# Queries made for one head of two batches, 512 columns at once, instead of two heads of one batch

## The chip, the cores and the metric

The program runs on one core of a Trainium2 chip. Its time is the device time of one launch in microseconds. Three runs of the kernel before gave 613.03, 613.40 and 614.61 us; their median is 613.4 us.

## The reference

Two layers follow each other on x of 4 batches x 256 tokens x 256 features, float32. Each sublayer is followed by a residual sum and a layer norm:

```
x = layernorm(x + attention0(x))   # latent queries and keys, rotary part, causal, 16 heads
x = layernorm(x + experts(x))      # 16 experts, the best 2 of each token, silu
x = layernorm(x + attention1(x))   # 16 query heads, 4 key heads, rotary, alibi, 30*tanh(s/30), causal
x = layernorm(x + x @ sign(w)*mean|w| + bias)
```

What the change touches are the queries of both attentions. In layer 0 they are rmsnorm(x @ Wq_a) @ Wq_b, with Wkv_b's key part folded into Wq_b by the kernel, so that a head's queries have 64 latent and 64 rotary features. In layer 1 they are x @ Wq, 128 features a head. In both, the rotary step then multiplies them by a cosine and adds a swapped copy times a sine. The scores are queries times keys; each head of each batch has its own causal softmax over 256 tokens.

## The kernel before

Everything stays in SBUF with features in partitions. The 16 heads are taken as 8 pairs p, the 4 batches as b, and one unit of work is m = 4p + b. `steps` (L363 to L375) writes the attention loop of every engine: bodies n = 4p + b from 0 to 31 (pair 0 and pair 7 written out, pairs 1 to 6 in a hardware loop), and three bodies behind them that only finish. TensorE, VectorE, ScalarE and GpSimd each run their own list of instructions in order and meet at semaphores.

A unit of queries (`pe_queries`, L478) fills one PSUM bank of 128 x 512: both heads of the pair, 256 tokens of one batch each. Products of float32 parts are made in passes (a high and a low part of each operand): 5 matmuls for each head in layer 0, 6 in layer 1, each of 256 moving columns. In body n TensorE first makes the scores of body n, then the query unit n + 3 (`ahead`, L377), then the context products and transposes of earlier bodies. The units 0 to 2 are made ahead of the loop (`pe_first_queries`). From unit 3 on all units use bank 7, so a unit waits until the one before has been read.

Layer 0, after a unit is in the bank: VectorE multiplies it by the cosine into qT (`dve_cos`, L1241) and twice 32 rows by the sine into `swapped` (L1247), and GpSimd adds the two in qT (`pool_sin`, L1524) and raises q_ready. In a body the softmax runs as: VectorE takes the row maxima (L1281, L1282) and neg_max (L1284, 128 x 4 values, both operands in SBUF), ScalarE makes four exp (L935), VectorE the reciprocals (L1292), GpSimd the normalisation (L1536) and right behind it the addition on qT of unit n + 3. TensorE transposes the result one body later. At b = 0 ScalarE also splits the next pair's weights into w_hi (L908) and GpSimd makes w_lo (L1223).

Layer 1, after a unit is in the bank: ScalarE copies it with halves of the partitions swapped (L917, L918), GpSimd multiplies that by the sine (L1528), VectorE multiplies by the cosine (L1241) and adds into q_sum (L1256). One body later ScalarE rounds q_sum to q_hi (L963) and VectorE takes the rest as q_lo (L1262), which raises q_ready. Ahead of q_lo VectorE makes k_hi and k_lo of the keys (L1271, L1273). In a body ScalarE makes tanh (L972), GpSimd adds the mask (L1546, L1547), ScalarE makes the exp (L983). w_lo is VectorE's here (L1223, at b = 0); TensorE needs it for the next pair's first unit, in the body b = 1.

The scores of body n wait for q_ready (L510, L558): the count n + 1, that is, the unit of the same number. Layer 0 reads qT, layer 1 reads q_hi and q_lo, all of them 128 x (2 heads) x (4 x 256 tokens).

Of the kernel before, what the change touches and what calls it, by code (L numbers as in the profile page):

```python
# [12 lines left out]
ALU = mybir.AluOpType  # L13
ACT = mybir.ActivationFunctionType
AX_X = mybir.AxisListType.X

P = 128
# [76 lines left out]
def raw(ap):  # L94

    return ap.bitcast(F32)
# [8 lines left out]
def build(nc, a, out, ctx):  # L105
# [205 lines left out]
    def pair_view(ap):  # L311
        return ap.rearrange("p (h t) -> p h t", h=2)
# [11 lines left out]
    def query_bank(p, b):  # L324

        return 4 + b if isinstance(p, int) and p == 0 and b < 2 else QRY
# [106 lines left out]
    def pe_project_out(eng, at):  # L433

        turn, parts = (0, PAIRS) if at["layer"] == 0 else (2, H)
        for t in range(NT):
# [32 lines left out]
            if t == 5 and at["layer"] == 1:  # L469
# [5 lines left out]
                                           ffn_bw[:, o, k * P:k * P + P], ident[:])  # L475
                mm.then_inc(ff["bwT_done"], 1)

    def pe_queries(eng, at, p, b):  # L478

        m = 4 * p + b  # L480
        if b == 0:
            eng.wait_ge(at["w_hi_done"], p + 1)
            eng.wait_ge(at["w_lo_done"], p + 1)
        if not (isinstance(p, int) and m < 3):
            if at["layer"] == 0:
                eng.wait_ge(at["sin_done"], m)
            else:
                eng.wait_ge(at["cos_done"], m)
                eng.wait_ge(at["swap_done"], m)
        some = slice(T * b, T * b + T)  # L490
        for h in range(2):
            dst, head = bank[:, query_bank(p, b), h * T:h * T + T], slice(h * P, h * P + P)
            if at["layer"] == 0:
                three_pass(eng, dst, w_hi[:, 0, head], w_lo[:, 0, head], latT_hi[:, 0, some], latT_lo[:, 0, some],
                           True, False)

                eng.matmul(dst, w_hi[:, 1, head], latT_hi[:, 1, some], start=False, stop=False,
                           skip_group_check=True)
                mm = eng.matmul(dst, w_lo[:, 1, head], latT_hi[:, 1, some], start=False, stop=True,
                                skip_group_check=True)  # L500
            else:
                for k in range(2):
                    mm = three_pass(eng, dst, w_hi[:, k, head], w_lo[:, k, head], xT_hi[:, k, some],
                                    xT_lo[:, k, some], k == 0, k == 1)
        mm.then_inc(at["q_done"], 1)

    def pe_attention0(eng, at):
        def body(p, b, n, lag, own, more):
            if own:
                eng.wait_ge(at["q_ready"], n + 1)  # L510
                if lag(2):
                    eng.wait_ge(at["exp_done"], n - 1)
                for h in range(2):
                    dst = bank[:, 2 * (b % 2) + h, :]
                    q = qT[:, h, T * b:T * b + T]
                    eng.matmul(dst[:, 0:T], q[:, P:T], keysT[:, 0, T * b:T * b + T],  # L516
                               start=True, stop=False, skip_group_check=True)
                    eng.matmul(dst[:, T:T + P], q[:, 0:P], keysT[:, 0, T * b:T * b + P],
                               start=False, stop=False, skip_group_check=True)

                    mm = eng.matmul(dst[:, P:3 * P], ident_bf[:], mask_bf[:],  # L521
                                    start=False, stop=True, skip_group_check=True)
                mm.then_inc(at["scores_done"], 1)
            if own and ahead(p, b, more):
                pe_queries(eng, at, *ahead(p, b, more))
            if lag(2):
                b2 = (b - 2) % B
                eng.wait_ge(at["probsT_copied"], n - 1)
                if lag(3):
                    eng.wait_ge(at["ctx_copied"], n - 2)  # L530
                values = [key_tok[:, 2 * b2 + j, 0:KVL] for j in range(2)]
                for h in range(2):
                    pt = probsT[:, b % 2, h, :]
                    dst = bank[64 * h:64 * h + 64, CTX, 0:T]
                    eng.matmul(dst, values[0], pt[:, 0:T], start=True, stop=False, skip_group_check=True)
                    mm = eng.matmul(dst[:, P:T], values[1], pt[:, T:T + P],
                                    start=False, stop=True, skip_group_check=True)
                mm.then_inc(at["ctx_done"], 1)
            if lag(1):
                eng.wait_ge(at["probs_ready"], n)  # L540
                if lag(2):
                    eng.wait_ge(at["probsT_copied"], n - 1)
                for h in range(2):
                    pr = probs[:, (b - 1) % 2, h, :]
                    dst = probsT_bank[:, h, :]
                    eng.transpose(dst[:, 0:P], pr[:, T:T + P], ident[:])
                    eng.transpose(dst[:, P:T], pr[:, 0:P], ident[:])
                    mm = eng.transpose(dst[:, T:T + P], pr[:, P:T], ident[:])
                mm.then_inc(at["probsT_done"], 1)

        steps(eng, body)

    def pe_attention1(eng, at):

        def body(p, b, n, lag, own, more):
            par = b % 2
            if own:
                eng.wait_ge(at["q_ready"], n + 1)  # L558
                eng.wait_ge(at["k_copied"], n + 1)
                if lag(2):  # L560
                    eng.wait_ge(at["capped"], n - 1)
                for tile in range(2):
                    dst = bank[:, 2 * par + tile, 0:(2 - tile) * T]
                    keys = slice(tile * P, tile * P + P)
                    queries = slice(T * b + tile * P, T * b + T)
                    three_pass(eng, dst, k_hi[:, par, keys], k_lo[:, par, keys], q_hi[:, :, queries],
                               q_lo[:, :, queries], True, False)

                    mm = eng.matmul(dst, alibi_keys[:, keys], alibi_queries[:, bass.ds(2 * p, 2), tile * P:T],  # L569
                                    start=False, stop=True, skip_group_check=True)  # L570
                mm.then_inc(at["scores_done"], 1)
# [385 lines left out]
    def act_query_hi(act, at, p, b):  # L957

        m = 4 * p + b
        act.wait_ge(at["q_summed"], m + 1)  # L960
        if not (isinstance(p, int) and p == 0):
            act.wait_ge(at["scores_done"], m - 3)
        act.activation(q_hi[:, :, T * b:T * b + T], pair_view(q_sum[:, b % 2, :]), ACT.Copy).then_inc(at["q_hi_done"], 1)  # L963

    def act_attention1(act, at):
        def body(p, b, n, lag, own, more):
# [265 lines left out]
    def dve_cos(dve, at, p, b):  # L1232
        m = 4 * p + b
        if at["layer"] == 0:
            dve.wait_ge(at["q_done"], m + 1)
        else:
            dve.wait_ge(at["swap_done"], m + 1)
            if not (isinstance(p, int) and m < 2):
                dve.wait_ge(at["q_ready"], m - 1)
        dst = qT[:, :, T * b:T * b + T] if at["layer"] == 0 else pair_view(q_sum[:, b % 2, :])  # L1240
        dve.tensor_tensor(dst, pair_view(bank[:, query_bank(p, b), :]), cos_rows(at["layer"]),  # L1241
                          ALU.mult).then_inc(at["cos_done"], 1)
        if at["layer"] == 0:
            if not (isinstance(p, int) and m < 2):
                dve.wait_ge(at["q_ready"], m - 1)
            for to, of in ((64, 96), (96, 64)):
                ins = dve.tensor_tensor(pair_view(swapped[to:to + 32, b % 2, :]),  # L1247
                                        pair_view(bank[of:of + 32, query_bank(p, b), :]),
                                        rope_sin[of:of + 32, 0:1, :].broadcast_to([32, 2, T]), ALU.mult)
            ins.then_inc(at["sin_done"], 1)  # L1250
# [8 lines left out]
    def dve_query_lo(dve, at, p, b):  # L1259

        dve.wait_ge(at["q_hi_done"], 4 * p + b + 1)
        dve.tensor_tensor(q_lo[:, :, T * b:T * b + T], pair_view(q_sum[:, b % 2, :]),  # L1262
                          raw(q_hi[:, :, T * b:T * b + T]), ALU.subtract).then_inc(at["q_ready"], 1)

    def dve_keys(dve, at, p, b):

# [251 lines left out]
    def pool_sin(pool, at, p, b):  # L1518
        m = 4 * p + b
        if at["layer"] == 0:  # L1520
            q = qT[:, :, T * b:T * b + T]
            pool.wait_ge(at["cos_done"], m + 1)
            pool.wait_ge(at["sin_done"], m + 1)
            pool.tensor_tensor(q, q, pair_view(swapped[:, b % 2, :]), ALU.add).then_inc(at["q_ready"], 1)  # L1524
        else:
            pool.wait_ge(at["swap_done"], m + 1)
            sw = pair_view(swapped[:, b % 2, :])
            pool.tensor_tensor(sw, sw, sin_rows(), ALU.mult).then_inc(at["sin_done"], 1)  # L1528
# [233 lines left out]
```

## Time and profile before

| what | us |
|---|---|
| median of three runs | 613.4 |
| the profiled execution, its own time | 610.71 |
| its span | 609.0 |
| TensorE matmuls busy | 506.7 (83%) |
| VectorE busy | 410.6 (67%) |
| ScalarE busy | 343.4 (56%) |
| GpSimd busy | 306.8 (50%) |
| layer 0's loop, bodies 0 to 31: start of the scores | 38.9 to 179.1 |
| layer 1's loop, bodies 0 to 31: start of the scores | 382.4 to 527.5 |

A matmul's busy time reaches from its start to the end of its result, so that neighbours overlap; the distance of two starts is what one costs. PEld is the weight load, which runs beside the matmul before it. The start of a body's scores is read at its first weight load: of keysT and qT (L516) in layer 0, of q_hi and k_hi (L394) in layer 1. A row with x2 merges two instructions of one kind that follow each other.

### The profile page before, as it was taken

To read this page: it belongs to the slowest core of one execution; us is meant where nothing else is said; L and a number is where in the kernel's file an instruction comes from. 1 tells how busy PE (TensorE), PEld (TensorE's weight loads), DVE (VectorE), ACT (ScalarE), POOL (GpSimd) and SP (SyncE) were. 2 spreads that over 40 slices of the span, in tenths; PEclk is the share of its full clock that TensorE was granted. 3 is DMA by queue.
4 is the path that set the end of the run, shared out by engine and by line. 5 is a ranking of instruction groups with operands and counts; after the bars stand their busy time and mean duration, and the time that the engine had idled before them with its cause. 6 is when DMAs were issued, how large, how long until landed. Compare 5 with 4: busy or idle time off the path is not lost. (4 is left out here: it accounts for less than half of the span.)

```text
span 609.0 us, 11070 instructions
## 1 busy us (share of the span) xinstructions
PE 506.7 (83%) x3497; PEld 442.3 (73%) x3513; DVE 410.6 (67%) x883; ACT 343.4 (56%) x737; POOL 306.8 (50%) x304
## 2 busy tenths in 40 slices
PE   5878999999986866278990479899999999879983
PEld 5567888888865866257870357788988888779983
DVE  2666888888863765424552766788888888585765
ACT  4534777676784432133340156888888888745313
POOL 5726686766752022532336555566666666570110
PEclk9997999999996967569996599999999999979997
DMA  8949995000000044246532200000000000400002
GB/s 282 350 127 399 425 427 223 0 0 0 1 1 1 1 150 195 70 153 225 160 114 86 78 0 1 2 2 0 0 0 0 0 0 1 138 18 2 1 1 69
DMA packets 19170, 56.34 MB, mean 93 GB/s; under 512 B 2773, under 2 KB 12507, under 8 KB 15419
## 3 DMA queue, kind: packets, MB, share of 16 engines
q1 hardware_dynamic: 15616, 47.41, 20.8%
q0 software_dynamic: 3520, 8.51, 4.3%
q8 instruction: 18, 0.29, 0.2%
q14 instruction: 16, 0.12, 0.1%
HBM read 27.98 MB, written 28.18 MB: 92 GB/s over the span
## 5 line engine op out<-in xcount | busy, mean ns | idle before, releaser
L935 ACT ACTIVATE probs<-bank,neg_max,q_scale 128x256 f32<-128x256 f32 (+1 forms) x128 | 63.6, 506 | 34.5 <-DVE neg_max L1284 34.4
L1536 POOL TENSOR_TENSOR probs<-probs,inv_sum 128x512 f32<-128x512 f32 x64 | 52.3, 839 | 44.7 <-DVE inv_sum L1292 44.4
L394 PE MATMUL bank<-xT_hi,w_hi 128*128 128x256 f32 (+1 forms) x144 | 46.2, 321 | 11.0 <-DVE w_lo L1223 4.8
L1546 POOL TENSOR_TENSOR probs<-probs,tables 128x256 f32<-128x256 f32 x32 | 26.8, 839 | 48.3 <-ACT probs L972 48.3
L1528 POOL TENSOR_TENSOR swapped<-swapped,tables 128x512 f32<-128x512 f32 x32 | 42.3, 1323 | 12.1 <-ACT swapped L918 12.1
L1247 DVE TENSOR_TENSOR swapped<-bank,tables 32x512 f32<-32x512 f32 x64 | 44.4, 693 | 1.4
L1524 POOL TENSOR_TENSOR qT<-qT,swapped 128x512 f32<-128x512 f32 x32 | 40.8, 1275 | 7.1 <-DVE swapped L1247 7.1
L395 PE MATMUL bank<-xT_lo,w_hi 128*128 128x256 f32 (+1 forms) x144 | 43.1, 299 | 0.0
L396 PE MATMUL bank<-xT_hi,w_lo 128*128 128x256 f32 (+1 forms) x144 | 43.1, 299 | 0.0
L1618 POOL DMA_INDIRECT slots<-x_tok,slot x16 | 15.8, 990 | 53.5 <-DVE slot L1453 49.8
L516 PE MATMUL bank<-keysT,qT 128*128 128x256 f32 x128 | 39.2, 389 | 0.7 <-ACT wo_full L1048 0.7
L396 PE MATMUL bank<-wo_hi,ctx_lo 128*128 128x256 f32 x128 | 39.4, 308 | 0.0
L394 PEld LDWEIGHTS bank<-xT_hi,w_hi 128*128 128x128 f32 x144 | 28.0, 194 | 14.9 <-issue 11.8
L1628 POOL DMA_DIRECT2D slots<-y_slot x31 | 16.8, 543 | 43.1 <-DVE y_slot L1491 42.4
L1649 POOL TENSOR_TENSOR x_tok<-x_tok,tables 128x512 f32<-128x512 f32 x8 | 15.0, 1888 | 41.0 <-PE bank L402 41.0
L730 PE MATMUL bank<-gu_all,xgT 128*128 x124 | 34.6, 404 | 0.0
L1547 POOL TENSOR_TENSOR probs<-probs,tables 128x256 f32<-128x256 f32 x32 | 34.0, 1061 | 0.0
L1262 DVE TENSOR_TENSOR q_lo<-q_sum,q_hi 128x512 fp32r<-128x512 f32 x32 | 25.4, 793 | 11.0 <-ACT q_hi L963 10.9
L972 ACT ACTIVATE probs<-bank 128x768 f32<-128x768 f32 x32 | 26.0, 813 | 11.7 <-PE bank L569 11.5
L1281 DVE TENSOR_REDUCE row_max<-bank 128x2 f32<-128x512 f32 x32 | 22.1, 691 | 14.4 <-PE bank L521 13.8
L1241 DVE TENSOR_TENSOR q_sum<-bank,tables 128x512 f32<-128x512 f32 x32 | 22.0, 689 | 13.5 <-ACT swapped L918 13.4
L983 ACT ACTIVATE probs<-probs 128x768 f32<-128x768 f32 x32 | 27.0, 843 | 6.9 <-POOL probs L1547 6.7
(272 smaller groups left out, 1899.1 us busy)
## 6 DMA issues: line engine op xcount, KB each, us to landing
slots<-wkv_raw SPq DMA_DIRECT2D x20, 1024.0 KB, 25.4
gu_all<-in_gate_up SPq DMA_DIRECT2D x4, 1024.0 KB, 9.2
xg<-slots SPq DMA_DIRECT2D x31, 128.0 KB, 2.1
slots<-y_slot POOLq DMA_DIRECT2D x31, 128.0 KB, 2.0
wvo_raw<-in_wvo SPq DMA_DIRECT2D x1, 2560.0 KB, 20.8
dn_all<-in_down SPq DMA_DIRECT2D x1, 2048.0 KB, 11.0
wq_full<-in_Wq SPq DMA_DIRECT2D x1, 2048.0 KB, 8.4
wo_raw<-in_Wo SPq DMA_DIRECT2D x1, 2048.0 KB, 8.2
```

Of the source, the lines that this page charges most:

```text
L394: eng.matmul(dst, s_hi, m_hi, start=start, stop=False, skip_group_check=True)
L395: eng.matmul(dst, s_hi, m_lo, start=False, stop=False, skip_group_check=True)
L396: return eng.matmul(dst, s_lo, m_hi, start=False, stop=stop, skip_group_check=True)
L516: eng.matmul(dst[:, 0:T], q[:, P:T], keysT[:, 0, T * b:T * b + T], start=True, stop=False, skip_group_check=True)
L730: mm = pe.matmul(bank[:, up_bank(k), 0:2 * FF], xgT[:, k % 2, c, :], gu_all[:, bass.ds(e, 1), c, :].rearrange("p e f -> p (e f)"), start=c ...
L935: ins = act.activation(probs[:, par, h, c0:c1], bank[:, 2 * par + h, c0:c1], ACT.Exp, bias=neg_max[:, par, i:i + 1], scale=q_scale[:, b, t ...
L983: act.activation(keys_first(par), keys_first(par), ACT.Exp, scale=30.0).then_inc(at["exp_done"], 1)
L1247: ins = dve.tensor_tensor(pair_view(swapped[to:to + 32, b % 2, :]), pair_view(bank[of:of + 32, query_bank(p, b), :]), rope_sin[of:of + 32, ...
L1524: pool.tensor_tensor(q, q, pair_view(swapped[:, b % 2, :]), ALU.add).then_inc(at["q_ready"], 1)
L1528: pool.tensor_tensor(sw, sw, sin_rows(), ALU.mult).then_inc(at["sin_done"], 1)
L1536: ins = pool.tensor_tensor(some, some, inv, ALU.mult)
L1547: pool.tensor_tensor(pr[:, 2 * T:3 * T], pr[:, 2 * T:3 * T], maskT, ALU.add).then_inc(at["masked"], 1)
```

## The change

A unit of queries now holds one head of the pair, b mod 2, for two batches, 2 (b div 2) and the next. Its passes are the same with 512 moving columns each, so there are half as many matmuls. Every engine that writes or reads a unit's columns takes the new place. The scores of a batch need both heads, hence two units: the bodies b = 0 and 1 wait for the units 4p and 4p + 1, the bodies b = 2 and 3 for 4p + 2 and 4p + 3. The order of the work and the number of semaphore increments stay.

```
+    def head_of(g):
+        return slice(g % 2 * P, g % 2 * P + P)
+    def batches_of(g):
+        return slice(2 * T * (g // 2), 2 * T * (g // 2) + 2 * T)
+    def queries_for(p, b):
+        return 4 * p + b // 2 * 2 + 2
 pe_queries:
-        some = slice(T * b, T * b + T)
-        for h in range(2):
-            dst, head = bank[:, query_bank(p, b), h * T:h * T + T], slice(h * P, h * P + P)
-...
+        dst, head, some = bank[:, query_bank(p, b), :], head_of(b), batches_of(b)
+...
 pe_attention0, pe_attention1:
-                eng.wait_ge(at["q_ready"], n + 1)
+                eng.wait_ge(at["q_ready"], queries_for(p, b))
 act_query_hi:
-            act.wait_ge(at["scores_done"], m - 3)
-        act.activation(q_hi[:, :, T * b:T * b + T], pair_view(q_sum[:, b % 2, :]), ACT.Copy)
+            act.wait_ge(at["scores_done"], m - b % 2 - 2)
+        act.activation(q_hi[:, b % 2, batches_of(b)], q_sum[:, b % 2, :], ACT.Copy)
 dve_cos:
-        dst = qT[:, :, T * b:T * b + T] if at["layer"] == 0 else pair_view(q_sum[:, b % 2, :])
+        dst = pair_view(qT[:, b % 2, batches_of(b)] if at["layer"] == 0 else q_sum[:, b % 2, :])
 dve_query_lo:
-        dve.tensor_tensor(q_lo[:, :, T * b:T * b + T], pair_view(q_sum[:, b % 2, :]),
-                          raw(q_hi[:, :, T * b:T * b + T]), ALU.subtract)
+        dve.tensor_tensor(q_lo[:, b % 2, batches_of(b)], q_sum[:, b % 2, :],
+                          raw(q_hi[:, b % 2, batches_of(b)]), ALU.subtract)
 pool_sin, layer 0:
-            q = qT[:, :, T * b:T * b + T]
-            pool.tensor_tensor(q, q, pair_view(swapped[:, b % 2, :]), ALU.add)
+            q = qT[:, b % 2, batches_of(b)]
+            pool.tensor_tensor(q, q, swapped[:, b % 2, :], ALU.add)
```

## Rows read from the trace of the kernel before

**Rows 1.** The page: busy time, and the slices (of TensorE and its granted clock).

```profile
PE 506.7 (83%) x3497; PEld 442.3 (73%) x3513; DVE 410.6 (67%) x883; ACT 343.4 (56%) x737; POOL 306.8 (50%) x304
...
PE   5878999999986866278990479899999999879983
...
PEclk9997999999996967569996599999999999979997
```

**Rows 2.** Stretches: busy time of PE, PEld, DVE, ACT, POOL, then clock, DMA, GB/s.

```profile
100.00:160.00 60.00, 59.93 (x463) 51.30 (x462) 51.02 (x96) 44.12 (x144) 43.41 (x45) 1.00 0.05 17
400.00:520.00 120.00, 117.39 (x897) 107.00 (x910) 100.16 (x183) 100.61 (x158) 80.20 (x77) 1.00 0.01 1
```

**Rows 3.** Timeline, layer 0, bodies 18 to 21, 26: start, us, engine, line, what.

```profile
122.75 0.30 PEld L516 LDWEIGHTS bank<-keysT,qT 128*128 128x128 f32 x2
125.65 0.16 DVE L1284 TENSOR_TENSOR neg_max<-row_max,q_minus 128x4 f32<-128x4 f32 x1
125.85 0.56 ACT L935 ACTIVATE probs<-bank,neg_max,q_scale 128x256 f32<-128x256 f32 x1 [1.05 <-DVE neg_max L1284]
127.08 0.30 PEld L516 LDWEIGHTS bank<-keysT,qT 128*128 128x128 f32 x2
129.79 1.27 POOL L1524 TENSOR_TENSOR qT<-qT,swapped 128x512 f32<-128x512 f32 x1
129.97 1.11 DVE L1284 TENSOR_TENSOR neg_max<-row_max,q_minus 128x4 f32<-128x4 f32 x1
131.12 0.56 ACT L935 ACTIVATE probs<-bank,neg_max,q_scale 128x256 f32<-128x256 f32 x1 [2.21 <-DVE neg_max L1284]
131.41 0.30 PEld L516 LDWEIGHTS bank<-keysT,qT 128*128 128x128 f32 x2
...
135.28 0.55 ACT L935 ACTIVATE probs<-bank,neg_max,q_scale 128x256 f32<-128x256 f32 x1
139.30 0.56 ACT L935 ACTIVATE probs<-bank,neg_max,q_scale 128x256 f32<-128x256 f32 x1 [0.98 <-DVE neg_max L1284]
...
158.07 0.30 PEld L516 LDWEIGHTS bank<-keysT,qT 128*128 128x128 f32 x2
```

**Rows 4.** Timeline, layer 1: w_lo, the queries behind it, q_lo and scores of b = 2.

```profile
426.52 0.19 PEld L394 LDWEIGHTS bank<-xT_hi,w_hi 128*128 128x128 f32 x1 [0.64 <-issue]
...
444.15 1.12 DVE L1223 TENSOR_TENSOR w_lo<-wq_full,w_hi 128x512 fp32r<-128x512 f32 x1
445.60 0.19 PEld L394 LDWEIGHTS bank<-xT_hi,w_hi 128*128 128x128 f32 x1 [0.59 <-issue]
448.23 0.68 DVE L1262 TENSOR_TENSOR q_lo<-q_sum,q_hi 128x512 fp32r<-128x512 f32 x1
448.80 0.19 PEld L394 LDWEIGHTS bank<-q_hi,k_hi 128*128 128x128 f32 x1
```

**Rows 5.** Timeline, ahead of layer 1's loop: first and last of two runs of matmuls.

```profile
371.62 0.28 PE L395 MATMUL bank<-xT_lo,w_hi 128*128 128x256 f32 x1
375.69 0.28 PE L396 MATMUL bank<-xT_hi,w_lo 128*128 128x256 f32 x1
377.20 0.39 PE L394 MATMUL bank<-wv_hi,xT_hi 128*128 128x512 f32 x1
381.05 0.39 PE L396 MATMUL bank<-wv_hi,xT_lo 128*128 128x512 f32 x1
```

**Rows 6.** Timeline, layer 0: additions of units 9 and 31, scores of bodies 8 and 30.

```profile
77.86 1.27 POOL L1524 TENSOR_TENSOR qT<-qT,swapped 128x512 f32<-128x512 f32 x1
78.75 0.30 PEld L516 LDWEIGHTS bank<-keysT,qT 128*128 128x128 f32 x2
...
174.41 1.28 POOL L1524 TENSOR_TENSOR qT<-qT,swapped 128x512 f32<-128x512 f32 x1
175.11 0.30 PEld L516 LDWEIGHTS bank<-keysT,qT 128*128 128x128 f32 x2
```

**Rows 7.** Timeline, layer 0: a sine product and the queries that waited for it.

```profile
131.71 1.40 DVE L1247 TENSOR_TENSOR swapped<-bank,tables 32x512 f32<-32x512 f32 x2
133.16 0.19 PEld L394 LDWEIGHTS bank<-latT_hi,w_hi 128*128 128x128 f32 x1 [0.23 <-DVE swapped L1247]
```

**Rows 8.** Timeline, layer 1: q_lo of unit 1, scores of body 0; behind body 30.

```profile
382.17 0.69 DVE L1262 TENSOR_TENSOR q_lo<-q_sum,q_hi 128x512 fp32r<-128x512 f32 x1
382.37 0.19 PEld L394 LDWEIGHTS bank<-q_hi,k_hi 128*128 128x128 f32 x1 [1.35 <-issue]
...
525.78 0.63 PE L584 MATMUL bank<-ident,ctx_tok 128*128 128x128 f32 x4 [1.11 <-ACT ctxT L987]
```

More of the change, by code:

```diff
@@ L489, in pe_queries @@
                 eng.wait_ge(at["swap_done"], m)
-        some = slice(T * b, T * b + T)
-        for h in range(2):
-            dst, head = bank[:, query_bank(p, b), h * T:h * T + T], slice(h * P, h * P + P)
[L493 to L504, printed above, removed]
+        dst, head, some = bank[:, query_bank(p, b), :], head_of(b), batches_of(b)
+        if at["layer"] == 0:
+            three_pass(eng, dst, w_hi[:, 0, head], w_lo[:, 0, head], latT_hi[:, 0, some], latT_lo[:, 0, some],
+                       True, False)
+            eng.matmul(dst, w_hi[:, 1, head], latT_hi[:, 1, some], start=False, stop=False,
+                       skip_group_check=True)
+            mm = eng.matmul(dst, w_lo[:, 1, head], latT_hi[:, 1, some], start=False, stop=True,
+                            skip_group_check=True)
+        else:
+            for k in range(2):
+                mm = three_pass(eng, dst, w_hi[:, k, head], w_lo[:, k, head], xT_hi[:, k, some],
+                                xT_lo[:, k, some], k == 0, k == 1)
         mm.then_inc(at["q_done"], 1)
@@ L557, in body @@
             if own:
-                eng.wait_ge(at["q_ready"], n + 1)
+                eng.wait_ge(at["q_ready"], queries_for(p, b))
                 eng.wait_ge(at["k_copied"], n + 1)
@@ L961, in act_query_hi @@
         if not (isinstance(p, int) and p == 0):
-            act.wait_ge(at["scores_done"], m - 3)
-        act.activation(q_hi[:, :, T * b:T * b + T], pair_view(q_sum[:, b % 2, :]), ACT.Copy).then_inc(at["q_hi_done"], 1)
+            act.wait_ge(at["scores_done"], m - b % 2 - 2)
+        act.activation(q_hi[:, b % 2, batches_of(b)], q_sum[:, b % 2, :], ACT.Copy).then_inc(at["q_hi_done"], 1)
     def act_attention1(act, at):
@@ L1261, in dve_query_lo @@
         dve.wait_ge(at["q_hi_done"], 4 * p + b + 1)
-        dve.tensor_tensor(q_lo[:, :, T * b:T * b + T], pair_view(q_sum[:, b % 2, :]),
-                          raw(q_hi[:, :, T * b:T * b + T]), ALU.subtract).then_inc(at["q_ready"], 1)
+        dve.tensor_tensor(q_lo[:, b % 2, batches_of(b)], q_sum[:, b % 2, :],
+                          raw(q_hi[:, b % 2, batches_of(b)]), ALU.subtract).then_inc(at["q_ready"], 1)
     def dve_keys(dve, at, p, b):
@@ L1520, in pool_sin @@
         if at["layer"] == 0:
-            q = qT[:, :, T * b:T * b + T]
+            q = qT[:, b % 2, batches_of(b)]
             pool.wait_ge(at["cos_done"], m + 1)
             pool.wait_ge(at["sin_done"], m + 1)
-            pool.tensor_tensor(q, q, pair_view(swapped[:, b % 2, :]), ALU.add).then_inc(at["q_ready"], 1)
+            pool.tensor_tensor(q, q, swapped[:, b % 2, :], ALU.add).then_inc(at["q_ready"], 1)
         else:
```

## The prediction

> **What bounds the kernel now.** I read the share of busy time first, then the busy slices, then the two attention loops by stretch, and only then single instructions. TensorE is the busiest engine of the span, and its slices stand at 9 exactly where the two attention loops run [rows 1]. By stretch it is busy 59.93 of 60.00 us in a piece of layer 0's loop and 117.39 of 120.00 us in layer 1's, at a granted clock of 1.00, its upper level of 2.4 GHz; VectorE is at 51.02 of 60 and 100.16 of 120 [rows 2]. No DMA matters there (share 0.05 and 0.01). So in both loops TensorE has no air: what shortens its instructions shortens the loop, and any new wait in front of it is paid. Both loops have 32 bodies (n = 4p + b), and a body takes 4.33 us in layer 0 when nothing waits (127.08 to 131.41) [rows 3]; in layer 1 four bodies take 445.60 - 426.52 = 19.08 us [rows 4].
>
> **What the change does to TensorE's own work.** A unit of queries was 10 matmuls (layer 0) or 12 (layer 1) of 256 columns and becomes 5 or 6 of 512: the same columns, half the instructions and half the weight loads. Two rows price it. In the burst at the start of layer 1, 34 steps of 256 columns take 375.69 - 371.62 = 4.07 us, 0.1197 each; right behind it, 17 steps of 512 columns take 381.05 - 377.20 = 3.85 us, 0.2265 each [rows 5]. One merged pair saves 2 x 0.1197 - 0.2265 = 0.013 us, a unit 0.065 us in layer 0 and 0.077 us in layer 1, and 32 + 32 units 4.5 us if all of it were on the path. The weight loads lie under the matmuls in both shapes, so they bring nothing more.
> The Trainium skill, page "TensorE: Matmul & The Clock Gate", section "Back-to-back issue gap", gives the gap as columns / 2.4 plus 2.5 ns, so 109 and 216 ns. The rows say 120 and 226. By the page a merged pair would save 2.5 ns and the whole change 0.9 us, by the rows 4.5 us; the measurement decides, but both say that the gain is small, and the page speaks against the change.
>
> **What else is edited.** VectorE's, ScalarE's and GpSimd's instructions keep their number and their 512 elements; only the place of the second half changes (contiguous instead of two strips 1024 apart). I cost that at zero: the addition on qT takes 1.27 us as it stands [rows 6]. ScalarE's copy to q_hi now waits for at most two bodies back while it stands behind the tanh of a later one, which has waited for more, so that wait never holds. Wo's DMA for layer 1 waits for the last query unit, which comes within 0.1 us of where it was. These cost nothing.
>
> **The new wait.** This is the part that counts. Body n used to need query unit n. Now units 4p and 4p+1 hold the two heads of batches 0 and 1, so an even body needs unit n+1, which was made one body later. TensorE issues unit n+3 in body n, so the lead shrinks from three bodies to two for every even body. Queued behind that wait on TensorE are the scores, the next unit of queries, the context matmuls and the transposes, and every other engine waits for those.
>
> *Layer 0.* Unit n+1 becomes ready when GpSimd's addition on qT ends. In body 8, unit 9's addition ends at 77.86 + 1.27 = 79.13, while the scores start at 78.75: 0.38 us too late. At body 30 it is 175.69 against 175.11, 0.58 too late [rows 6]. Over the even bodies from 4 on, the addition ends after the scores' start in seven of 14 (8, 10, 16, 18, 24, 26, 30: 0.38, 0.19, 0.37, 0.18, 0.36, 0.20, 0.58 us), and in three more it is only 0.10 us ahead. So the wait is real, but its size is no sum of these, since a late body moves what comes after it.
> To size it I carry the loop forward with intervals read from four bodies [rows 3]; s is the start of a body's scores on TensorE, E the start of its first exp on ScalarE. (a) VectorE is ready for neg_max 2.90 us after s (122.75 to 125.65). (b) GpSimd's addition of a body runs from E + 3.94 to E + 5.21 (E = 125.85, addition 129.79 to 131.06). (c) If the next body's neg_max (L1284) comes while this addition runs, it takes 1.11 us instead of 0.16 and ends with it; the next E is then 131.12 - 125.85 = 5.27 us after this one. (d) If it comes while GpSimd's normalisation runs, just ahead of the addition, it waits for that, and the next E is 139.30 - 135.28 = 4.02 us later. Together with TensorE's own waits for the sin product and for w, these four carried over bodies 10 to 18 give the starts of the scores of before within 0.05 us.
> Now the change. An even body's scores start at E(two before) + 5.21 + l, where l is the delay from the end of the addition to TensorE. Its neg_max is ready 2.90 later, at E + 8.11 + l. The odd body between has its E at E + 4.02 (case d), so its own addition runs from E + 7.96 to E + 9.23, and the even body's neg_max falls into it for any l between -0.15 and 1.1 us. So case (c) follows case (d) in every pair, and the loop locks in a cycle of 4.02 + 5.27 = 9.29 us per two bodies. Before, eight bodies take 158.07 - 122.75 = 35.32 us [rows 3], 8.83 per two. TensorE's saving disappears in its wait. Started from body 4, the cycle catches at body 8, 0.5 us late. From there to body 26 nine pairs take 83.6 instead of 158.07 - 78.75 = 79.3 us, and to body 30 two more take 18.6 instead of 17.0 [rows 3, 6]: with the 0.5 that is 6.4 us. Behind body 30 nothing blocks neg_max, and its E comes 3.1 instead of 3.4 us after s, 0.3 back; the rounding of the intervals is worth as much again. I take +5.8 us for layer 0, between +4.5 and +6.5. The front (three units before the loop) gives 0.2 us back.
> The Trainium skill, page "SBUF — State Buffer", section "SBUF: two separate sides", says that a VectorE instruction with two SBUF inputs and a GpSimd one that reads SBUF exclude each other for a whole instruction. The trace agrees with 1.11 against 0.16 us on L1284. By that rule the cycle is a property of the program and not of this execution.
>
> *The delay l.* The trace of before has no case of scores waiting for q_ready. Nearest below: VectorE's sin product ends at 133.11 and TensorE loads weights at 133.16, 0.05 us [rows 7]. Nearest above: w_lo of layer 1 ends at 444.15 + 1.12 = 445.27 and the load behind it starts at 445.60, 0.33 us [rows 4]; there more waits on register values are queued behind the one that held, as they are in front of the scores. I take 0.3 in the loops. Layer 0's cycle doesn't depend on it, layer 1's does.
>
> *Layer 1.* Three of four bodies are unhurt: for b = 0, q_lo of the needed unit ends 0.7 us ahead of the scores. For b = 2 it doesn't: q_lo ends at 448.23 + 0.68 = 448.91, the scores start at 448.80 [rows 4], and it is so six times (0.06 to 0.12 us). The chain from w_lo to that q_lo is VectorE's own and isn't changed, so from w_lo's end to these scores takes 448.91 + l - 445.27 = 3.64 + l instead of 3.53, and the other three bodies of the four give 3 x 0.077 back: -0.12 + l, with l = 0.3 +0.18 us per four bodies, six times +1.1 us (from -0.4 with l = 0.05 to +1.3 with 0.33). At its start, body 0 needs unit 1, whose q_lo ends at 382.86 while the scores started at 382.37 [rows 8]: +0.5 us, and the tanh, the split of w and so the fourth body hang on it; body 2 +0.1. At its end body 30 is late by 0.7 us, but TensorE idles 1.11 us behind its scores for ScalarE anyway [rows 8], which hides it; two or three cheaper units give 0.2 back. Layer 1: +1.5 us, from 0 to +1.8.
>
> **Sum.** +5.8 - 0.2 + 1.5 = +7.1 us. Against the profiled execution's own 610.71 us (span 609.0) that is 617.8; the median of the runs shown is 613.4, 2.7 above it, so I forecast 620.5 us. A measurement tells about 0.3% of this kernel, 1.8 us, from no change.
>
> **Rivals.** First: the wait holds where it is late, but no cycle forms; the seven shortfalls of layer 0 are paid once each, 2.3 us plus seven times 0.2, less 28 x 0.065 = 1.8 of cheaper units, +1.9, and with layer 1's +1.5 the time is 616.8 us. For it: in the trace of before, blocked and free bodies alternate and the backlog dies away. Against: the arithmetic above needs no luck. Chance 0.17.
> Second: the same, with l near 0.05, as behind the sin product: layer 0 +0.9, layer 1 -0.2, 614.1 us. Chance 0.12.
> Third, on the other side: the waits retune the loop so that neg_max always comes free, ahead of GpSimd's addition. Body 18 shows it: its neg_max took 0.16 us and its addition ended 131.06 - 122.75 = 8.31 us after its scores began [rows 3], while TensorE needs 2 x (4.33 - 0.065) = 8.53 us for two bodies. Then no wait holds and eight bodies take 34.1 instead of 35.3 us: three times that between bodies 4 and 28, -3.6 us, with the front's -0.2 and layer 1's +1.5 611.1 us. It decides from the point where an even body's neg_max comes before E + 7.96 above, which wants l below -0.15. Chance 0.09.
> A transfer or the clock as a bound I leave out: neither moves with the change.
>
> **How the numbers follow.** Forecast 0.62, with a range of its own of 618.3 to 622.5; the rivals 0.17, 0.12, 0.09. The range reaches down to the second rival and up past the forecast's end: 614.0 to 622.6. Slower by over 0.3% (above 615.2) is the forecast and nearly all of the first rival, 0.77; within 0.3% is the second with a rest of the first, 0.14; faster (below 611.6) is the third, 0.09.
>
> **What would show it.** In layer 0's loop TensorE idles about 0.6 us ahead of every even body's scores, released by GpSimd's addition on qT; the scores of even bodies stand 9.3 us apart, the last even body's near 181 us; L1284 takes about 1 us in every even body. In layer 1 the scores of b = 2 wait 0.2 to 0.4 us for q_lo, four bodies take 19.2 us, and body 0 starts late by 0.5. Matmuls of 512 columns in the query units stand 0.226 us apart. The prediction is wrong if the even bodies keep 8.7 to 8.8 us, or if TensorE's idle time there stays below 0.2 us.

## The result

| kernel | median | lowest to highest | runs |
|---|---|---|---|
| before | 612.37 us | 609.47 to 614.75 | 16 |
| after | 620.88 us | 614.89 to 622.77 | 16 |

After over before is 1.0138, with a 95% interval of 1.0115 to 1.0162: slower by 7.0 to 9.9 us. The profiled execution of after took 621.52 us, span 619.8 (before 610.71 and 609.0).

The page of after: busy time, the slices of TensorE and of its granted clock, and the group of layer 0's scores (busy time and mean ns | idle time ahead of the group, and what ended most of it).

```profile
PE 512.5 (83%) x3161; PEld 422.1 (68%) x3161; DVE 416.0 (67%) x883; ACT 343.8 (55%) x737; POOL 307.0 (50%) x304
...
PE   5879999999986958268992289799999999969983
...
PEclk9997999999997977568997589999999999979997
...
L526 PE MATMUL bank<-keysT,qT 128*128 128x256 f32 x128 | 40.5, 398 | 3.8 <-POOL qT L1534 3.2
```

The stretches of [rows 2], same columns:

```profile
100.00:160.00 60.00, 58.42 (x377) 43.69 (x375) 52.29 (x90) 41.00 (x131) 41.22 (x43) 1.00 0.05 17
400.00:520.00 120.00, 117.34 (x751) 97.92 (x750) 100.68 (x183) 99.49 (x156) 78.82 (x76) 1.00 0.00 0
```

There are 336 matmuls fewer in the records (352 by the code), as intended, and no time was won. In layer 0 TensorE, which had 0.07 us of idle time in 60 [rows 2], now has 1.58, and the scores have a new releaser: GpSimd's addition on qT.

Layer 0's loop, the timeline that answers to [rows 3] and [rows 6]. First the scores of body 8, then bodies 18 to 20, then the scores of bodies 30 and 31:

```profile
79.40 0.30 PEld L526 LDWEIGHTS bank<-keysT,qT 128*128 128x128 f32 x2 [0.48 <-issue]
...
126.08 0.30 PEld L526 LDWEIGHTS bank<-keysT,qT 128*128 128x128 f32 x2 [0.51 <-POOL qT L1534]
128.79 1.27 POOL L1534 TENSOR_TENSOR qT<-qT,swapped 128x512 f32<-128x512 f32 x1
128.97 1.10 DVE L1294 TENSOR_TENSOR neg_max<-row_max,q_minus 128x4 f32<-128x4 f32 x1
130.11 0.56 ACT L945 ACTIVATE probs<-bank,neg_max,q_scale 128x256 f32<-128x256 f32 x1 [2.21 <-DVE neg_max L1294]
130.37 0.30 PEld L526 LDWEIGHTS bank<-keysT,qT 128*128 128x128 f32 x2
133.49 0.62 DVE L1294 TENSOR_TENSOR neg_max<-row_max,q_minus 128x4 f32<-128x4 f32 x1
134.05 1.27 POOL L1534 TENSOR_TENSOR qT<-qT,swapped 128x512 f32<-128x512 f32 x1
134.14 0.57 ACT L945 ACTIVATE probs<-bank,neg_max,q_scale 128x256 f32<-128x256 f32 x1 [0.98 <-DVE neg_max L1294]
135.45 0.30 PEld L526 LDWEIGHTS bank<-keysT,qT 128*128 128x128 f32 x2 [0.49 <-issue]
...
182.03 0.30 PEld L526 LDWEIGHTS bank<-keysT,qT 128*128 128x128 f32 x2 [0.59 <-POOL qT L1534]
...
185.44 0.30 PEld L526 LDWEIGHTS bank<-keysT,qT 128*128 128x128 f32 x2
```

Read it as a circle. The scores of body 18 start at 126.08. Its neg_max starts 2.89 us later, while the addition of body 17 runs, and ends with it (130.07 against 130.06). The exp, the normalisation and body 18's own addition (unit 21) hang on it; this addition ends at 134.05 + 1.27 = 135.32, and the scores of body 20, which need unit 21, start at 135.45. Two bodies take 135.45 - 126.08 = 9.37 us. Every pair from body 8 to body 30 takes 9.29 to 9.38. A row released by "issue" here is the same wait: its start stands 0.13 us behind the addition. Body 8 is 0.65 us later than before, body 30 is 6.92, body 31 is 6.30.

Layer 1, answering to [rows 4] and [rows 8]: the scores of body 0, one group of w_lo, queries, q_lo and the scores of b = 2, and the scores of body 31.

```profile
391.82 0.68 DVE L1272 TENSOR_TENSOR q_lo<-q_sum,q_hi 128x512 fp32r<-128x512 f32 x1
392.73 0.19 PEld L394 LDWEIGHTS bank<-q_hi,k_hi 128*128 128x128 f32 x1 [2.15 <-issue]
...
454.67 1.13 DVE L1233 TENSOR_TENSOR w_lo<-wq_full,w_hi 128x512 fp32r<-128x512 f32 x1
456.12 0.19 PEld L394 LDWEIGHTS bank<-xT_hi,w_hi 128*128 128x128 f32 x1 [0.60 <-issue]
458.75 0.68 DVE L1272 TENSOR_TENSOR q_lo<-q_sum,q_hi 128x512 fp32r<-128x512 f32 x1
459.49 0.19 PEld L394 LDWEIGHTS bank<-q_hi,k_hi 128*128 128x128 f32 x1
...
538.50 0.19 PEld L394 LDWEIGHTS bank<-q_hi,k_hi 128*128 128x128 f32 x1
```

Here the scores of b = 2 are the row at 459.49, 0.06 us behind q_lo's end (459.43). From body 0 to body 31 the loop takes 145.77 us, before 145.10 (382.37 to 527.47).

### The profile page after: what moved, and what is told of

It reads as the page before. It is cut to its first block and busy times, and to the rows that moved or that the text cites. A ratio compares the mean times of both kernels' runs of the same rounds, so it can differ in the third digit from the quotient of the medians.

```text
span 619.8 us, 10376 instructions
## 1 busy us (share of the span) xinstructions
PE 512.5 (83%) x3161; PEld 422.1 (68%) x3161; DVE 416.0 (67%) x883; ACT 343.8 (55%) x737; POOL 307.0 (50%) x304
## 5 line engine op out<-in xcount | busy, mean ns | idle before, releaser
L394 PE MATMUL bank<-xT_hi,w_hi 128*128 128x512 f32 x80 | 35.7, 447 | 11.1 <-DVE w_lo L1233 4.8
L526 PE MATMUL bank<-keysT,qT 128*128 128x256 f32 x128 | 40.5, 398 | 3.8 <-POOL qT L1534 3.2
L396 PE MATMUL bank<-xT_hi,w_lo 128*128 128x512 f32 x80 | 32.5, 407 | 0.0
L395 PE MATMUL bank<-xT_lo,w_hi 128*128 128x512 f32 x80 | 32.3, 404 | 0.0
L394 PE MATMUL bank<-q_hi,k_hi 128*128 128x512 f32 x64 | 30.3, 474 | 2.2 <-DVE q_lo L1272 2.2
```

The source lines that it names most:

```text
L394: eng.matmul(dst, s_hi, m_hi, start=start, stop=False, skip_group_check=True)
L395: eng.matmul(dst, s_hi, m_lo, start=False, stop=False, skip_group_check=True)
L396: return eng.matmul(dst, s_lo, m_hi, start=False, stop=stop, skip_group_check=True)
```

## The experiments

Seven kernels, each timed in five rounds beside the kernel before. "Body 30" is the start of its scores in layer 0; the last column is layer 1 from the scores of body 0 to those of body 31; both from one profiled execution. The ratios are taken against the runs of the kernel before that were timed beside each kernel; their medians are 612.51 us for wait_only, new_layer1, after_neg_free and before_neg_free, and 612.23 us for the other three.

| kernel | median, us | ratio to before (95%) | body 30 | layer 1's loop |
|---|---|---|---|---|
| before | 612.37 | | 175.11 | 145.10 |
| after | 620.88 | 1.0138 (1.0115 to 1.0162) | 182.03 | 145.77 |
| wait_only | 618.26 | 1.0114 (1.0074 to 1.0154) | 181.75 | 146.47 |
| new_layer0 | 619.09 | 1.0106 (1.0064 to 1.0149) | 181.94 | 145.07 |
| new_layer1 | 612.11 | 1.0013 (0.9982 to 1.0045) | 174.14 | 145.74 |
| after_neg_free | 610.66 | 0.9986 (0.9961 to 1.0011) | 173.93 | 147.30 |
| before_neg_free | 607.79 | 0.9938 (0.9914 to 0.9961) | 171.81 | 145.08 |
| wait_neg_free | 611.56 | 0.9998 (0.9974 to 1.0023) | 174.36 | 146.43 |
| after_add_first | 614.54 | 1.0044 (1.0023 to 1.0066) | 177.90 | 147.27 |

Layer 0 of new_layer1 is the same program as in the kernel before. Its body 30 starts at 174.14 us and its body 31 at 179.86, against 175.11 and 179.14 before; its granted clock was 0.83 from 175 to 185 us, against 1.00. Such a start can differ by 0.7 to 1.0 us between two executions of the same work, so a smaller difference needs the durations of single bodies behind it.

### wait_only: the new wait without the new units

```
 pe_attention0, pe_attention1 of the kernel before:
-                eng.wait_ge(at["q_ready"], n + 1)
+                eng.wait_ge(at["q_ready"], queries_for(p, b))
```

> The kernel before with one edit: the scores of both layers wait for queries_for(p, b) units, as after the change; the query units keep their two heads of one batch and their 256 columns. Theory (the cycle of wait, exp and blocked neg_max sets layer 0): even bodies of layer 0 stand 9.3 us apart from body 8 on, body 30's scores start at 181.5 to 182.5 us, L1284 takes 1.0 to 1.1 us in every even body, time 620 to 622 us, equal to the changed kernel within 1 us. Rival (the 512-column matmuls or the new places of the queries are what costs): body 30 stays near 175 us and the time at 612 to 613 us.

Its timeline in layer 0, bodies 18 to 20:

```profile
125.77 0.30 PEld L520 LDWEIGHTS bank<-keysT,qT 128*128 128x128 f32 x2 [0.47 <-POOL qT L1528]
128.48 1.26 POOL L1528 TENSOR_TENSOR qT<-qT,swapped 128x512 f32<-128x512 f32 x1
128.66 1.10 DVE L1288 TENSOR_TENSOR neg_max<-row_max,q_minus 128x4 f32<-128x4 f32 x1
130.10 0.30 PEld L520 LDWEIGHTS bank<-keysT,qT 128*128 128x128 f32 x2
133.18 0.62 DVE L1288 TENSOR_TENSOR neg_max<-row_max,q_minus 128x4 f32<-128x4 f32 x1
133.74 1.27 POOL L1528 TENSOR_TENSOR qT<-qT,swapped 128x512 f32<-128x512 f32 x1
135.15 0.30 PEld L520 LDWEIGHTS bank<-keysT,qT 128*128 128x128 f32 x2 [0.47 <-issue]
```

This is the same circle as in after, row for row, with body 30 at 181.75. No matmul, layout or buffer differs from the kernel before, so the wait alone makes the loss in layer 0's loop. The time missed the expectation: 618.26 us lies below 620 to 622 and 2.6 us below after, which was to be equal within 1 us. The profiled executions differ by 3.3 us, and between the two layers' loops alone by 3.5 (207.29 us in after, 203.82 here), which the section on the prediction comes back to. One of its six runs took 764.99 us at a granted clock of 0.64, against 0.92 in the others; it isn't in the ratio and isn't explained.

### new_layer0 and new_layer1: where the loss sits

The edit is the change of the kernel after, made in one layer only; the other layer keeps its units and waits.

> The change made in layer 0 alone; layer 1 keeps its units of both heads of one batch and its old waits. Theory: the whole loss sits in layer 0's cycle of neg_max and GpSimd's addition, which this kernel has in full: the scores of body 30 start at 181.7 to 182.1 us as in the changed kernel, two bodies take 9.30 to 9.38 us, neg_max takes 1.0 to 1.1 us in every even body, and four bodies of layer 1 take 19.07 us as before; the time is 619 to 621 us, beside 612.4 before. Rival: the losses of the two layers are shared, and layer 1's late start and its wait for q_lo bring 1.5 us or more: 617 to 618.5 us here.

> The change in layer 1 alone; layer 0 keeps its units of one batch. Theory: layer 0 as in the kernel before (body 30 at 175 us), layer 1's loop 0.6 to 0.8 us longer from body 0 to 31 (four bodies 19.2 instead of 19.07), time +0.5 to +1.5 us, 613 to 614 us. Rival (layer 1 carries a good part of the 8.5 us): time 616 us or more.

Layer 0 alone has the whole circle (body 30 at 181.94, against 182.03 with both layers changed) and 1.0106 of the time. Layer 1 alone comes out at 1.0013 with an interval around 1: its loop costs 0.64 us more, and the timing can't tell that from nothing (612.11 us, just under the expected 613 to 614). In the traces the losses add up: each loop takes within 0.1 us what it takes when both layers are changed. The times agree with that (0.0106 and 0.0013, against 0.0138), but their intervals are too wide to exclude a shared microsecond.

### after_neg_free and before_neg_free: the circle cut

Both kernels have one edit: q_minus is copied once, ahead of layer 0's loop, into spare columns of two PSUM banks, and neg_max reads it there. Its result is the same, but one of its operands is no longer in SBUF. The two operands also change places in the instruction.

```
+    def minus_of(par):
+        return bank[:, 2 * par, 3 * P:3 * P + 2 * B].rearrange("p (b t) -> p b t", b=B)
 neg_max of layer 0:
+                minus_of(par)[:, b, :].unsqueeze(2).broadcast_to([P, 2, 2]),
                 row_max[:, par, :].rearrange("p (t h) -> p t h", t=2),
-                q_minus[:, b, :].unsqueeze(2).broadcast_to([P, 2, 2]),
...
 VectorE, ahead of layer 0's loop:
+        for par in range(2):
+            dve.tensor_copy(minus_of(par), q_minus[:]).then_inc(su["q_scaled"], 1)
...
```

> The changed kernel with neg_max's factor q_minus copied once into spare columns of the two PSUM banks of the scores, so that L1284's counterpart reads one operand from PSUM and one from SBUF. Theory: it no longer stops for GpSimd's addition (0.2 us in every body instead of 1.04 to 1.10 in even ones), exp starts 3.1 us after the scores (3.6 where b = 0), the pairs of bodies take 8.6 to 8.9 us instead of 9.33, body 30 starts at 174 to 176 us instead of 182, time 613 to 615 us. Rival (the wait alone costs, neg_max's stop is a side effect of it): pairs stay above 9.2 us, time 619 to 621 us.

> The kernel before with the same edit of neg_max. Theory: TensorE sets layer 0's loop alone, 4.33 us a body (8.66 a pair instead of 8.83), body 30 at 173 to 174 us instead of 175.1, time 610 to 611.5 us against 612.4. Rival (neg_max's stops are hidden in the kernel before): body 30 within 0.3 us of 175.1, same time.

The instruction by itself in after, then in after_neg_free (count: duration in ns as minimum/median/maximum, first and last start):

```profile
L1294 DVE TENSOR_TENSOR neg_max<-row_max,q_minus x32: 161/622/1211, 41.9 to 188.3; 128x4 f32<-128x4 f32 x32
```

```profile
L1299 DVE TENSOR_TENSOR neg_max<-bank,row_max x32: 160/162/164, 42.2 to 180.5; 128x4 f32<-128x4 f32 x32
```

In the timeline of after_neg_free neg_max runs in the middle of an addition and isn't held:

```profile
122.05 0.30 PEld L530 LDWEIGHTS bank<-keysT,qT 128*128 128x128 f32 x2 [0.25 <-POOL qT L1543]
...
129.08 1.27 POOL L1543 TENSOR_TENSOR qT<-qT,swapped 128x512 f32<-128x512 f32 x1
129.25 0.16 DVE L1299 TENSOR_TENSOR neg_max<-bank,row_max 128x4 f32<-128x4 f32 x1
...
139.52 0.30 PEld L530 LDWEIGHTS bank<-keysT,qT 128*128 128x128 f32 x2 [0.26 <-POOL qT L1543]
```

With the same wait, body 30 comes at 173.93 instead of 182.03, and the change is back at the time of before. What is left of the wait is 0.25 us in every fourth body (122.05, 139.52). In the kernel before, the same edit takes 3.30 us off body 30 (2.33 against the same layer 0 in new_layer1), and every body from 3 to 28 takes 4.32 to 4.34 us. It gives 607.79 us, ratio 0.9938 (0.9914 to 0.9961): the best kernel of this study, better than before and after. Both expectations had the mechanism right and the gain too small: after_neg_free was expected at 613 to 615 us and body 30 at 174 to 176, before_neg_free at 610 to 611.5 us and body 30 at 173 to 174; it started at 171.81.

### wait_neg_free: what the larger units are worth

The kernel before with the waits of wait_only and the neg_max of before_neg_free. It differs from after_neg_free in the units alone.

> The kernel before with two edits: the changed kernel's waits for queries (even bodies wait for unit n + 1), and layer 0's neg_max with its row of q_minus in PSUM. The units of queries stay at 256 columns. Theory: against the changed kernel with the same neg_max (610.66 us) only TensorE's cheaper units are missing, and these are worth what the loops show, 0.04 us a unit in layer 0 and 0.02 in layer 1, about 2 us in all with the front: 611.5 to 613.5 us; in layer 0's loop the unhurt bodies take 4.32 to 4.34 us instead of 4.29 to 4.31, the body b = 2 of each four still waits 0.2 to 0.3 us for the addition on qT, and the last even body's scores start near 174.5. Rival: the cheaper units are worth what the prediction took (0.065 and 0.077 us a unit, 4.5 us in all): 615 us, and the scores of body 30 near 175.5.

Body 30 at 174.36 against 173.93; an unhurt body takes 4.32 to 4.34 us against 4.29 to 4.31. The merged matmuls do save, about 0.5 us over layer 0's loop: 0.43 at body 30, 0.48 at body 31, and 17.47 against 17.56 us for four bodies (from body 18 to 22). In the times, 611.56 and 610.66 us, the intervals of the ratios overlap. Against before_neg_free the wait costs 2.55 us at body 30 and 1.95 at body 31 (178.08 against 176.13) with the circle cut. With the circle whole it costs 6.64 and 6.03 (wait_only, 181.75 against 175.11 and 185.17 against 179.14).

### after_add_first: the unit ready earlier

```
 pool_attention, each body:
+            if own and at["layer"] == 0 and ahead(p, b, more):
+                pool_sin(pool, at, *ahead(p, b, more))
             if own and at["layer"] == 0:
                 pool_normalise(pool, at, n, b % 2)
-            if own and ahead(p, b, more):
+            if own and at["layer"] == 1 and ahead(p, b, more):
                 pool_sin(pool, at, *ahead(p, b, more))
```

> The changed kernel, with GpSimd's addition on qT put ahead of the normalisation in every body of layer 0. Theory: the even bodies' wait for q_ready is gone, since the addition ends about 1.9 us earlier, but there is no slack for it to give: the normalisation ends 0.9 us or more later, TensorE's transposes wait for it instead, with the next body's scores queued behind them, and neg_max still meets a GpSimd instruction. From the rows of the changed kernel the normalisation ends 4.9 us after the first exp and the scores two bodies on start 1.1 us behind the transposes' first load, so two bodies take 9.1 to 9.5 us, and the time is 618 to 624 us. Rival: the wait for the unit is what costs, whatever stands in front of it; once the unit is early the loop returns to the 8.8 us per two bodies of the kernel before or below, and the time is 610 to 613 us.

Part of its timeline, from an addition and the normalisation behind it to the next scores:

```profile
129.68 1.28 POOL L1534 TENSOR_TENSOR qT<-qT,swapped 128x512 f32<-128x512 f32 x1 [1.62 <-DVE swapped L1257]
130.91 1.61 POOL L1546 TENSOR_TENSOR probs<-probs,inv_sum 128x512 f32<-128x512 f32 x2
131.60 0.37 DVE L1294 TENSOR_TENSOR neg_max<-row_max,q_minus 128x4 f32<-128x4 f32 x1
132.58 0.14 PEld L556 LDWEIGHTS bank<-ident,probs 128*128 128x128 f32 x1 [0.34 <-POOL probs L1546]
133.18 0.30 PEld L526 LDWEIGHTS bank<-keysT,qT 128*128 128x128 f32 x2
```

Theory and rival both missed. The direction of the theory holds: no scores wait for q_ready any more, and the transposes wait for the normalisation instead, 0.34 to 0.36 us in every body, with another 0.36 to 0.37 us ahead of the context products. Its size does not: a body takes 4.47 us, two 8.94, not 9.1 to 9.5. I had carried over the exp starting about 4 us behind the scores as in after's even bodies. But neg_max now meets the first of the normalisation's two instructions (1.04 us by itself, from 130.91 to 131.95) near its end and is held to 0.37 us instead of 1.1, so the exp starts 3.3 us behind the scores. The rival's 8.8 us isn't reached either. At 614.54 us this is 6.3 us better than after and 2.2 us worse than before.

## Why the prediction was right

620.5 us was forecast and 620.88 measured. The mechanism was the forecast one, but the agreement to 0.4 us is in part luck. The forecast stood on 613.4 us, the median of three runs; over 16 runs it is 612.37, 1.0 lower. The rise was forecast at 7.1 us and measured at 8.5, 1.4 higher, and the loops explain only 7.4 of it (*The sum*, below).

*The lock in layer 0 was right in kind and place.* It catches at body 8, as the carried-over intervals said. In wait_only and new_layer0, whose first bodies fall a little differently, neg_max is held for 1.03 us as early as body 4. The intervals gave 4.02 + 5.27 = 9.29 us per two bodies; from body 8 to body 30 the trace has eleven times (182.03 - 79.40) / 11 = 9.33. Case (d) measures 4.03 to 4.04. Case (c), read before from one body with b = 3, is 5.26 to 5.27 into the bodies b = 2, but 5.35 to 5.36 into the bodies 8, 12, 16, 20 and 24 (b = 0). This and the 0.65 us at body 8 (0.5 forecast) are the 0.5 us by which body 30 came later than forecast (+6.9 against +6.4). Behind it 0.6 us are given back, and as much was taken off in the forecast, in two halves of which only one, the earlier exp, had a row. So body 31 is late by 6.3 (forecast +5.8, upper bound +6.5), give or take the 0.7 us that separate two executions of the old layer 0 there. The first rival, the same wait without a cycle, is excluded by the traces of after and wait_only, and after_neg_free shows what that rival would have looked like. The third, that the wait retunes the loop so that neg_max comes free, is excluded too: neg_max takes 1.04 to 1.11 us in every even body from 6 to 28. Two of the rivals' sums have slips that change nothing: the first adds seven waits of 0.2 us where the working took 0.3 for l, and the first and second leave out the front's 0.2.

*The saving on TensorE was mis-sized.* I took 0.065 us per unit in layer 0 and 0.077 in layer 1. Layer 1's units in the loop say 0.02. Here is the unit of before, then that of after, each from its first matmul to the next instruction on TensorE, and last the second and the eighteenth matmul of after's three units ahead of the loop:

```profile
440.35 0.36 PE L394 MATMUL bank<-xT_hi,w_hi 128*128 128x256 f32 x1
440.56 0.28 PE L395 MATMUL bank<-xT_lo,w_hi 128*128 128x256 f32 x1
...
441.74 0.28 PE L396 MATMUL bank<-xT_hi,w_lo 128*128 128x256 f32 x1
441.86 0.60 PE L584 MATMUL bank<-ident,ctx_tok 128*128 128x128 f32 x4
```

```profile
450.89 0.49 PE L394 MATMUL bank<-xT_hi,w_hi 128*128 128x512 f32 x1
451.22 0.40 PE L395 MATMUL bank<-xT_lo,w_hi 128*128 128x512 f32 x1
...
452.15 0.39 PE L396 MATMUL bank<-xT_hi,w_lo 128*128 128x512 f32 x1
452.38 0.60 PE L594 MATMUL bank<-ident,ctx_tok 128*128 128x128 f32 x4
```

```profile
381.50 0.40 PE L395 MATMUL bank<-xT_lo,w_hi 128*128 128x512 f32 x1
385.17 0.39 PE L396 MATMUL bank<-xT_hi,w_lo 128*128 128x512 f32 x1
```

1.51 us became 1.49. Inside the unit a step of 256 columns is 0.118 us and one of 512 is (452.15 - 451.22) / 4 = 0.2325, where [rows 5] had 0.1197 and 0.2265. 2 x 0.118 - 0.2325 leaves 0.004 us a pair, not 0.013, and the first pair leaves nothing: its step is 0.33 us, where 0.21 + 0.118 were two. The 512-column rows of [rows 5] were of another operation, with the roles of x and the weights exchanged, but that isn't all of it: in the burst of after, the query units themselves stand (385.17 - 381.50) / 16 = 0.2294 us apart, which leaves 0.010 us a pair. So the error was to carry rows of a long burst into units of 5 or 6; why the steps differ, no run here shows. In layer 0's loop, from unit 6 on, a unit went from 1.35 to 1.39 us to 1.32 to 1.36 in after and 1.32 to 1.35 in after_neg_free. The forecast for the three units ahead of the loop, 0.2 us, came to 0.1 (3.64 to 3.56 us), and body 0 starts no earlier (39.03 against 38.85). In all the units saved about 1 us: the 0.9 us that the prediction worked out from the page is nearer to it than the 4.5 from the rows.

*The delay l was mis-sized too.* I took 0.3 us in the loops between the wait's end and TensorE's first load. It is 0.05 to 0.13 in layer 0 and 0.06 in layer 1, the lower of my two bounds; only body 0 of layer 1, with 0.23, is nearer to the upper. Layer 0's cycle doesn't depend on l, as the working said, so the second rival had the right l and the wrong price: with a small l there is the same cycle.

*Layer 1 came out a little cheaper, since the two errors oppose each other.* Four bodies take 19.19 to 19.22 us instead of 19.07: +0.12 to +0.15 where +0.18 was forecast. The start stands 0.7 us later behind the q_lo of unit 0 (+0.5 forecast), the loop adds 0.67, and behind body 31 0.2 come back: +1.1, for +1.5. From w_lo's end to the scores of b = 2 it takes 459.49 - 455.80 = 3.69 us instead of 3.53; with 3 x 0.02 us given back by the units that is +0.10 per four bodies, near what was measured.

*The sum.* Layer 0 (6.3) and layer 1 (1.1) together explain 7.4 us of the 8.5 between the medians, inside the measured 7.0 to 9.9. The profiled executions differ by 10.8. From body 31 of layer 0 to body 0 of layer 1 after took 207.29 us against 203.23. Of these 4.1 us 0.7 are layer 1's start. The other 3.4 don't follow from the change: the same stretch took 202.62 and 202.51 in after_neg_free and after_add_first, which carry the whole change. Over all nine kernels it runs from 202.08 to 207.29, with 203.82 in wait_only, 205.57 in new_layer1 and 205.96 in new_layer0, where the first layers differ and the code of this stretch doesn't. It holds the experts; the granted clock over the whole stretch was 0.80 in before and 0.79 in after. What sets its length these runs don't show.

*The signs.* The even bodies' 9.3 us, neg_max's 1 us, layer 1's 19.2 us and body 0's delay came as listed. In layer 1 the scores of b = 2 start 0.32 us behind the matmul before them (0.14 in before), a wait of 0.18 us, just under the 0.2 to 0.4 forecast. TensorE's idle time ahead of the even scores is 0.42 to 0.59 us by the weight loads (0.6 forecast) and 0.18 to 0.35 by the matmuls, close to the 0.2 that I had named as the mark of being wrong: the sign should have said by which rows it is read. The steps of 512 columns are 0.2325 us in the loop, not 0.226.

## What to carry to other kernels

Merging units along the moving dimension couples consumers that were apart: count the lead of each consumer in bodies before counting saved instructions. Here the larger units were worth about 1 us (0.5 in layer 0's loop, 146.47 - 145.77 = 0.7 in layer 1's), and one body of lead cost about 7 (6.0 and 146.47 - 145.10 = 1.4 in wait_only). A wait of a few tenths can lock a loop into a longer period when it moves a small instruction under a long one of another engine; carrying two bodies forward with intervals from the trace finds the period, while adding up the shortfalls does not. Price a matmul by rows of its own operation in a group of its own length. When a tiny instruction has a duration many times its minimum, look for what runs on GpSimd at that moment.

## What the runs showed of the hardware

**The hold on neg_max is a matter of where its operands lie.** With both operands in SBUF, 128 x 4 elements took up to 1.21 us in after when a GpSimd instruction ran, and ended with it. With one of the two in PSUM they took 0.160 to 0.164 us in all 32 bodies, under the same GpSimd instructions. The Trainium skill, page "SBUF — State Buffer", section "SBUF: two separate sides", tells of the exclusion of the two engines and names two SBUF inputs as its condition for such an instruction. These runs agree: one operand in PSUM was enough to escape it. I had used the rule to explain a cost and hadn't seen in it a gain of 0.6% for the kernel before.

**After the same pause of TensorE one execution went on at the full clock and another at half.** Here are two stretches of after_neg_free at the start of layer 1, then the same two of after, placed alike behind their body 0 (columns as in [rows 2], the granted clock third from the end):

```profile
384.00:387.80 3.80, 1.93 (x10) 1.50 (x10) 3.34 (x5) 3.23 (x5) 3.02 (x4) 1.00 0.01 2
387.80:391.00 3.20, 3.20 (x15) 3.09 (x14) 2.15 (x4) 2.03 (x3) 1.88 (x2) 0.50 0.00 0
```

```profile
396.50:400.30 3.80, 1.92 (x11) 1.50 (x10) 3.34 (x5) 3.24 (x5) 3.03 (x4) 1.00 0.00 0
400.30:403.50 3.20, 3.20 (x23) 2.74 (x22) 2.96 (x7) 2.03 (x3) 1.92 (x2) 1.00 0.01 3
```

Both were busy for half of the first stretch, with one pause of about 1.9 us. In after_neg_free the next 3.2 us then ran at a clock of 0.50, the level of 1.2 GHz, 15 matmuls instead of 23, and in after at 1.00. This is why layer 1's loop shows 147.30 us in one and 145.77 in the other, though its code is the same: body 1 took 7.67 us instead of 6.45 and body 2 took 4.90 instead of 4.59, and the rest agree. after_add_first has it too (clock 0.58 from 391 to 395 us, body 1 at 7.58); the other seven executions have body 1 at 6.26 to 6.45. The pause alone doesn't bring it, and why one execution is granted the full clock and the other isn't, these runs don't say. It is a reason for reading single stretches beside whole times.
